# Causal attention between two feed-forward blocks: another set of whole tiles and new slots for the stages around them

## The reference

```
x = x + 0.5 * ffn(layernorm(x))
x = x + attention(layernorm(x))
x = x + 0.5 * ffn(layernorm(x))

ffn(z)       = z @ W.T + b + (z @ V_r) @ C.T
attention(z) : 16 heads of width 16, q, k, v = split(z @ W_attn)
               s = q @ k.T / 4, for keys j <= i only
               p = (s*s + 1 if s > 0 else 1 - s/100) / 1000     (for s >= -100)
               y = (p @ v) @ W_proj
```

## Time and profile before

| | us |
|---|---|
| median of 3 runs | 1784.87 |
| profiled execution, time | 1781.97 |
| profiled execution, first to last instruction | 1780.2 |
| TensorE busy (matmuls) | 1610.6 |
| ScalarE busy | 1364.4 |
| VectorE busy | 1328.6 |
| GpSimd busy | 1319.1 |

### The profile page before, as it was taken

The page is one execution under the profiler, slowest core; times in us unless marked ns, Lnnn a source line. Parts: engine busy times, 40 slices in busy tenths (PEclk is TensorE's granted clock), DMA queues, the critical chain, the costliest instruction groups (busy, mean ns, idle before and its releaser), DMA issues.

```text
span 1780.2 us, 67010 instructions
## 1 busy us (share of the span) xinstructions
PE 1610.6 (90%) x27158; PEld 834.3 (47%) x27158; DVE 1328.6 (75%) x3272; ACT 1364.4 (77%) x2178; POOL 1319.1 (74%) x1415
## 2 busy tenths in 40 slices
PE   5788889998999999999999999999999989998884
PEld 3444444454545454554545455554545443434342
DVE  4776787778787878787787878778787778786661
ACT  2355668898888888888787887888897879797660
POOL 3456568888988878788897878788796768685652
PEclk9999999999999999999999999999999999999997
DMA  3453343324334252443334152433425141413102
GB/s 95 159 169 120 109 144 89 116 73 123 92 115 127 60 166 72 133 112 110 111 107 138 55 170 77 124 94 110 130 80 147 46 118 41 118 41 94 40 29 64
DMA packets 156857, 183.17 MB, mean 103 GB/s; under 512 B 22140, under 2 KB 129788, under 8 KB 155012
## 3 DMA queue, kind: packets, MB, share of 16 engines
q1 hardware_dynamic: 156548, 178.82, 34.4%
HBM read 101.38 MB, written 76.30 MB: 100 GB/s over the span
## 4 chain that ended last, share of the span: by engine, by line
PE 55%; DVE 16%; ACT 12%; issue 6%; POOL 6%; DMA 3%; SPq 1%; ACTq 0%; POOLq 0%; DVEq 0%
PE y_ps L1079 20%; PE bank L1079 16%; PE score L1079 16%; DVE rp L1012 9%; ACT rp L910 5%; ACT rp L926 3%; POOL rp L807 3%; PE bank L1105 3%; DVE lin L1018 2%; DMA x1c<-x_scratch 2%; POOL z L769 1%; DVE bnst_ln L1037 1%; ACT rp L930 1%; ACT lin L916 1%; POOL rp L782 1%
## 5 line engine op out<-in xcount | busy, mean ns | idle before, releaser
L1012 DVE TENSOR_SCALAR rp<-score 128x512 f32<-128x512 f32 (+2 forms) x1728 | 944.3, 574 | 287.0 <-PE score L1079 284.2
L807 POOL TENSOR_TENSOR rp<-rp 128x1024 f32<-128x1024 f32 (+1 forms) x416 | 757.3, 1829 | 57.9 <-DVE rp L1012 46.1
L1079 PE MATMUL score<-qs,ks 96*32 96x512 bf16 (+3 forms) x10240 | 725.1, 350 | 54.2 <-DVE lin L1018 22.7
L1079 PE MATMUL y_ps<-rp,vt 128*16 128x512 f32 (+3 forms) x5120 | 598.7, 533 | 27.2 <-POOL rp L807 11.3
L910 ACT ACTIVATE rp<-score 128x512 f32<-128x512 f32 (+1 forms) x832 | 463.5, 602 | 201.5 <-PE score L1079 199.5
L1079 PEld LDWEIGHTS score<-qs,ks 96*32 96x32 bf16 x10240 | 303.4, 96 | 432.7 <-DVE rp L1012 146.0
L926 ACT ACTIVATE rp<-rp,rise 128x1024 f32<-128x1024 f32 (+1 forms) x416 | 466.4, 1155 | 0.4 <-POOL rp L782 0.4
L782 POOL TENSOR_SCALAR_AFFINE_SELECT rp<-rp 128x256 f32<-128x256 f32 (+1 forms) x384 | 186.4, 487 | 291.3 <-DVE rp L1012 163.4
L930 ACT ACTIVATE rp<-rp 128x1024 f32<-128x1024 f32 (+2 forms) x224 | 291.8, 1308 | 83.9 <-POOL rp L782 57.2
L1018 DVE SCALAR_TENSOR_TENSOR lin<-score,slope_mask 128x128 f32<-128x128 f32 x768 | 215.3, 280 | 0.0
L1079 PEld LDWEIGHTS y_ps<-rp,vt 128*16 128x16 f32 x5120 | 143.2, 96 | 116.4 <-issue 38.3
(11 more groups left out here) (79 smaller groups left out, 1292.1 us busy)
## 6 DMA issues: line engine op xcount, KB each, us to landing
qs<-part_scratch SPq DMA_DIRECT2D x384, 64.0 KB, 2.4
ks<-part_scratch SPq DMA_DIRECT2D x384, 64.0 KB, 2.4
part_scratch<-parts SPq DMA_DIRECT2D x12, 1536.0 KB, 5.6
state_scratch<-st_new SPq DMA_DIRECT2D x16, 528.0 KB
st<-state_scratch SPq DMA_DIRECT2D x64, 132.0 KB
x_sb<-in_L_attn_x_dram SPq DMA_DIRECT2D x16, 512.0 KB, 4.5
x_scratch<-x SPq DMA_DIRECT2D x16, 512.0 KB, 5.6
qT_scratch<-qkT SPq DMA_DIRECT2D x16, 512.0 KB, 5.6
```

Source lines behind the costliest of these rows:

```text
L807: pool.tensor_tensor(half, half, half, ALU.mult).then_inc(squared["pool"], 1)
L1012: nc.vector.tensor_scalar(rp[T % RP_BUFS][:, 2 * u + v, off:CH], score[H % S_BUFS][:, v, off:CH], 0.0, RISE, ALU.max, ALU.add).then_inc(ra ...
L1079: return nc.tensor.matmul(*args, start=start, stop=stop, skip_group_check=True)
```

## The change

The set of whole tiles is written as a list, still 14 of 40. Tiles 2, 9, 11, 16, 22, 39 become shared; tiles 1, 6, 17, 26, 31, 34 become whole. In the tables of stages A, B and C eight starts move.

```
-WHOLE = OFF_DIAG[3::4] + [t for t in DIAG if TILES[t][2] >= 2 * P]
+WHOLE = [1, 3, 6, 10, 17, 20, 23, 26, 28, 31, 33, 34, 35, 38]

-A_FULL = {"z1T": (32, 33), "ffn": (36, 40), "z2T": (61, 63), "ln1": 10, "ln2": 45}
-B_FULL = {"qT": (0, 7), "k": (8, 12), "v": (16, 20), "kT": (45, 57), "state": (49, 59, 61, 63)}
-C_FULL = {"proj": (22, 26), "ln3": 30, "z3T": (69, 69), "out": (72, 76)}
+A_FULL = {"z1T": (32, 33), "ffn": (36, 40), "z2T": (63, 63), "ln1": 10, "ln2": 48}
+B_FULL = {"qT": (0, 5), "k": (8, 12), "v": (15, 19), "kT": (39, 55), "state": (49, 59, 61, 63)}
+C_FULL = {"proj": (22, 26), "ln3": 32, "z3T": (69, 69), "out": (72, 76)}
```

## The result

The changed kernel took 1767.43 us (median of 4 runs, 1766.43 to 1770.31) beside 1787.35 us (4 runs, 1782.54 to 1791.44) for the kernel before: ratio 0.990, 95% interval 0.987 to 0.993. Measured again later with more runs (`after_again`) it was 1767.74 us against 1782.55 us: 0.992, interval 0.990 to 0.994. So it is faster by 0.8 to 1.0%, where 1767 us (-1.0%) was forecast. The total agrees; the parts do not, as the rest of this document shows. The profiled execution took 1770.31 us, with a span of 1768.6 us and a mean granted clock of 0.983, as before.

What follows compares the result with a forecast made beforehand. TensorE was taken as the bound, with 8.6 us of standstill per iteration open. Terms summed to -3.2 us per iteration, -1.7 kept; -22 us in total, taken as -18, giving 1767 us (-1.0%), range 1742 to 1798.

Steps and rivals of the forecast that it cites:

- sign of being right: No waits before tile 24 or for tile 31's square, early tile 27 lin, iteration 99 to 99.5 us, engine loads shifted.
- tiles 22 to 26: VectorE's wait before tile 24 goes, half the next stays, tile 26 whole adds 0.5 us; net -1.2 us per iteration.
- tile 28: ScalarE's lin of tile 27 comes early, -1.0 us; VectorE's 0.4 wait grows to 0.5; net -0.9 us.
- tiles 31 to 36: Tile 31's wait for GpSimd's square goes, -0.85 us; VectorE late at whole tiles 33 to 35, +0.8; net -0.1 us.
- tiles 0 to 2: ScalarE's square of tile 0 comes earlier, its 0.6 us wait goes; tile 2's 0.4 may stay; net -0.6 us.
- tiles 15 to 18 (19): Tile 16 shared and later ln3 take 1.9 us from VectorE ahead of tile 17; -0.4 us.
- z2T: Slot 63: second z2T waits for VectorE to empty the state bank, covered by the first; 0, at most +0.3 us.
- What bounds the kernel: TensorE needs 92.3 us undisturbed of a 100.9 us iteration; only its 8.6 us of standstill can move.
- rival 4: GpSimd overloaded in slots 40 to 47, TensorE waits for squares of tiles 22 to 24; +1 us, 1774 us; chance 0.12.
- rival 2: VectorE becomes the bound at tiles 26 to 28 and 33 to 35; +1.8 us per iteration, 1810 us; chance 0.16.
- Iterations 12 to 14: They have the tile set but few stages; -1 us each, -3 in all.
- A little over half: Share kept of the summed -3.2 us, as removed waits run into the next: -1.7 us for iterations 1 to 11.

Runs made afterwards that it cites:

- set_ln2_qtv_z2t65: set_ln2_qtv with the second z2T at slot 65 instead of 63; 1747.48 us, ratio 0.981 to the kernel before.
- kt45: The changed kernel with the first kT back at slot 45 instead of 39; 1762.37 us, ratio 0.987 to the kernel before.
- swap22_26: The changed kernel with tile 22 whole again and tile 26 shared; 1768.77 us, ratio 0.990 to the kernel before.
- set_only: The kernel before with the new set of whole tiles and the old slots; 1791.84 us, ratio 1.004.
- set_ln2: set_only with ln2 at 48 instead of 45 and z2T at 63 and 63 instead of 61 and 63; 1763.80 us, ratio 0.988 to the kernel before.
- kt45_z2t65: kt45 with the second z2T at slot 65 instead of 63; 1760.87 us, ratio 0.987 to the kernel before.
- z2t61: The changed kernel with the first z2T back at slot 61 instead of 63; 1796.16 us, ratio 1.007 to the kernel before.
- set_ln2_qtv: The changed kernel with kT at 45 and 57 instead of 39 and 55, ln3 at 30 instead of 32; 1750.29 us, ratio 0.983 to the kernel before.
- set_only_shift4: set_only with each layer norm's shift as four one-column instructions with one SBUF input each; 1785.90 us, ratio 1.001 to the kernel before.

## Why the prediction was right and where it was wrong

The time came out as forecast, for reasons only partly those forecast, and its closeness is in good part luck. The forecast summed -22 us over iterations 1 to 14 and took -18. In the two profiles these iterations gave -8.6, and 2.8 of that is the stop in iterations 7 and 8. The prediction's own sign of being right, an iteration of 99 to 99.5 us, did not come: it was 100.3. The rest came from outside the sum. In the runs of `after_again` the mean granted clock was 0.985 for the changed kernel (mean of 6 runs) and 0.981 for the kernel before (17 runs); with half the length of a low-clock stretch as its cost, I estimate that at 7 to 8 of the 14.8 us between the medians. What raised it is not shown. By its own steps, for a full iteration (iterations 4 to 10, from start to start, us):

| step | forecast | measured |
|---|---|---|
| tiles 22 to 26 | -1.2 | scores -1.6; values of tiles 20, 21, 23, 24: +2.4 |
| tile 28 | -0.9 | -1.4, and values of tiles 26, 28: +0.8 |
| tiles 31 to 36 | -0.1 | -0.2 |
| tiles 0 to 2 | -0.6 | -0.6 |
| tiles 15 to 18 (19) | -0.4 | 0 |
| `z2T` | 0, at most +0.3 | +0.4 (0.68 for 0.26) |
| waits under 0.2 elsewhere | 0 | -0.3 |
| kept of the sum; length of the iteration | -1.7 | -0.65 |

- *What bounds the kernel.* Right. TensorE's undisturbed 92.3 us is the same in every variant, and all differences lie in its standstill and its clock. ScalarE gained 8.6 us of work and set nothing: the time fell. In `set_ln2_qtv_z2t65` ScalarE is busy 85.8 of 97.5 us and the iteration is the shortest.
- *Tiles 22 to 26.* The waits before tiles 24 and 25 went, as forecast, and the new ones stayed below what was allowed for (tile 23 0.41, tile 26 0.37). The error was to count only scores and VectorE. Tile 22's square and `kT`'s first half both went to GpSimd in slots 40 to 48, and GpSimd's lateness appears at *values*, three tiles later. It is what rival 4 described, put at +1 us and given 12 in 100. It measured 1.42 at tile 24 in the seven iterations with stages A and C and in iteration 11, which has C without A, and nothing in 1 to 3, much as that rival said; smaller waits for ScalarE's squares of tiles 20, 21 and 23 came with it. `kt45` and `swap22_26` show it from two sides. The forecast should have held this rival for the likeliest; its arithmetic (7.4 to 11.4 us of work in 8 slots) already stood in the text.
- *Tile 28.* Direction right, size too small: also VectorE's 0.4 went in iterations 4 to 10, where I had let it grow to 0.5. What the sum did not have is that `ln2`'s move also takes the shift, 0.49 us beside a square in iteration 6, from this place: with it there `set_only` waits 2.4 us, without it `set_ln2` 1.1. That VectorE's 0.4 is gone too in iterations 4 to 10 fits with TensorE coming later there, held up at tile 24's values: in iterations 1 to 3, without that hold, 0.39 of it stays. This is argued and not shown. (`swap22_26` can't settle it, since there ScalarE raises tile 26 again.)
- *Tiles 31 to 35.* Right for the net in full iterations, and rival 2, a chain on VectorE, did not come there: the wait at tile 36 is unchanged at 0.19 us. It comes when `z2T` is out of the way (`kt45_z2t65`), as 0.3 to 0.5, and in iterations 1 to 3 of the changed kernel itself, where tile 36's scores wait 0.8 us and waited 0 before. This is the row of iteration 1, 0.51 from start to start:

```profile
336.98 0.40 PE L1079 MATMUL score<-qs,ks 96*32 96x512 bf16 x4 [0.33 <-DVE lin L1018]
```

- *Tiles 0 to 2.* Right in both parts: the 0.6 us before tile 0's values are gone, the 0.4 us of tile 2 stays.
- *Tiles 15 to 18.* Wrong. The wait before tile 18 went, and 0.49 us came at tile 19, one tile further, again VectorE's: the queue there is what it was, only later.
- *`z2T`.* Wrong by its cover. The first `z2T` (0.59 us) does not hide VectorE's emptying; it is queued behind tile 31's first half, and that costs 0.68 us. The forecast also took the three slots of `ln2` for harmless to `z2T`; the first `z2T` waits for GpSimd's normalisations as soon as TensorE comes earlier (`kt45`, 0.4 us). `z2t61` shows what the other choice costs.
- *Iterations 12 to 14.* Forecast -1 each, measured +2.4 in all three, +2.35 of it in iteration 12, where the kernels with the new set have 98.9 us or more and the three without it 97.2 or 97.3. Waits for VectorE grew there before tiles 30 and 31 (1.8 for 0), tile 8 (1.4 for 0.3), tile 28 (1.5 for 0.8, half of which was ScalarE's) and tiles 2 and 3 (1.7 for 0.3), more than went at tiles 0 and 1 (0.9) and at the values of tiles 27 to 29 (1.0). No experiment took it apart further.
- *"A little over half".* Halving the sum of single waits was too mild for full iterations (-0.65 of -3.2 came), and about right for iterations 1 to 3 (-1.5). No part of the argument had the stop in iteration 7, the two ends and the clock, which made up the rest of the total.

Not separated: in a full iteration `set_ln2_qtv` is 2.5 us shorter than the changed kernel, and `kt45` alone gives 0.8 of that. The other 1.7 belong to `kT`'s second start (57 for 55) and `ln3` (30 for 32) together. Since iterations 1 to 3, which have `kT` but no `ln3`, do not differ (93.8 against 93.7), `ln3` is the likelier cause. The traces show it for one part. Tile 24's values come in slot 54, ahead of either second start of `kT`, so between these two kernels only `ln3` can differ there: in full iterations `kt45` waits 0.56 and `set_ln2_qtv` nothing, in iteration 11 1.43 and nothing. The rows of iteration 11, `kt45` first:

```profile
1296.16 1.05 PE L1079 MATMUL y_ps<-rp,vt 128*16 128x512 f32 x8 [1.23 <-POOL rp L807]
```

```profile
1282.51 1.06 PE L1079 MATMUL y_ps<-rp,vt 128*16 128x512 f32 x8
```

For the other 1.1 us it is argued and not shown.

## What to carry to other kernels

When load moves from one engine to another, write out every queue it lands in over the next slots, for the values as well as for the scores, before pricing the wait that it removes: here the set alone cost 0.4%, the slots alone 0.2%, and the pair of `ln2` and `z2T` together with the set gained 1.2%. Move a producer and its consumer together, and try a bundle of moves one by one: two of the moves in this change (`kT`, `ln3`) held back about as much as the change gave (`ln3` was never tried by itself), and without them the kernel is 1.7% faster instead of 0.8 to 1.0% (1.9% with the second `z2T` moved too).

## What the runs showed of the hardware

**VectorE waits for GpSimd's running instruction.** L971 reads two tensors from SBUF. With GpSimd idle it takes 0.16 us. Otherwise it ends 0.01 to 0.02 us after a GpSimd instruction, in all of the 38 longer cases of the kernel before and the 38 of `set_only`: in the kernel before, one began 0.03 us after a square (L807) of 1.89 us and took 1.88 us. That is the instruction that was running when it started, or, where that one ended at once, the next: in `set_only` it began 0.04 us before the end of a square, and took 1.17 us beside L487's 1.14. The form with one tensor and a scalar of each partition took 201 to 216 ns beside the same instructions. The Trainium skill, page "SBUF — State Buffer", section "Who interferes with whom", says a VectorE instruction with two SBUF inputs contends with a GpSimd instruction that reads SBUF, and that contention for the port pair they share is an exclusive lock. The trace agrees, with these numbers. The prediction weighed the sharing only on GpSimd's squares beside VectorE's raises, which read PSUM, and found nothing; the instruction that pays is a small one on VectorE.

**Stretches at half clock behind short standstills.** In `set_only`, iterations 5, 7, 8 and 9 took 102.5 to 103.1 us and the others of the kind 101.1 to 101.2. Each of the four holds a stretch of 3.4 us at about half clock (the row below, from iteration 5), right behind the standstill of TensorE before tile 28 (here 2.08 us of idle time of the weight loads before 713.49):

```profile
714.00:717.40 3.40, 3.08 (x20) 0.83 (x20) 1.75 (x4) 2.01 (x2) 3.27 (x4) 0.54 0.05 13
```

```profile
713.49 0.13 PEld L1079 LDWEIGHTS score<-qs,ks 96*32 96x32 bf16 x4 [2.08 <-DVE rp L1012]
```

In `set_ln2` and `set_only_shift4`, where that wait is 1.3 and 0.6 us shorter, no iteration from 1 to 11 has such a stretch. That the standstill is the cause is not shown beyond this coincidence: iterations 6 and 10 of `set_only` have the same standstill (1.81 us from start to start) and keep the full clock, while iteration 8, with 1.48, does not. In `z2t61` TensorE stands 2.3 or 2.4 us before the first `z2T` in each of iterations 1 to 10, and such a stretch begins within 1.5 us of it in iterations 1, 3 and 9 only.
